# Two layers of row scatters that skip nodes which are no edge's source, with the tables zeroed during the sorts

## The reference, cut to what matters

```python
loops = jnp.arange(N); src = concat([edge_index[0], loops]); dst = concat([edge_index[1], loops])
deg = segment_sum(ones, dst, N); dinv = rsqrt(deg); norm = dinv[src] * dinv[dst]
for l in range(3):
    h = x @ W[l].T
    agg = segment_sum(h[src] * norm[:, None], dst, N) + b[l]
    xn = (agg - mean(agg, 0)) * rsqrt(var(agg, 0) + 1e-5)
    x = relu(gamma[l] * xn + beta[l])
x = layernorm(x0 + x)
x = layernorm(x + messages(x, src, dst, edge attributes))
```

## Time and profile before

| | us |
|---|---|
| device time, median of 3 runs | 1859.32 |
| the three runs | 1864.98, 1859.32, 1850.93 |
| the profiled execution: span | 1724.5 |
| the profiled execution: device time of its own | not listed |
| the sorts, from the span's start to the last issue on SyncE's queue | 0 to 178.5 |
| the page's slices | 43.1 each |

### The profile page before, as it was taken

How to read it: one execution, slowest core, us unless ns; L and a number is a source line. 1 busy time by engine, 2 the same in 40 slices (tenths; PEclk the granted TensorE clock), 3 DMA queues, 4 the chain that set the end, 5 groups by cost and what they waited for, 6 DMA issues and landing times. The chain is left out here.

```text
span 1724.5 us, 26873 instructions
## 1 busy us (share of the span) xinstructions
PE 1368.7 (79%) x8020; PEld 1171.3 (68%) x8020; DVE 1213.7 (70%) x3500; ACT 905.4 (53%) x1796; POOL 889.3 (52%) x865
## 2 busy tenths in 40 slices
PE   4566599999988799999979999964444459999941
PEld 3455488788877688888868888853333358888831
DVE  7257566655656577777758777857877669999873
ACT  3462234433434577777566666635665644444374
POOL 5770567777774678777552343302333533433226
PEclk8799699999999899999989999975666679999955
DMA  2000697777867676777664566448998733333113
GB/s 62 2 2 2 220 315 253 256 257 253 271 226 261 209 246 246 249 258 258 222 202 158 202 206 207 151 186 290 337 343 326 302 85 91 85 93 90 55 45 142
DMA packets 129803, 330.41 MB, mean 192 GB/s; under 512 B 33772, under 2 KB 66020, under 8 KB 126870
## 3 DMA queue, kind: packets, MB, share of 16 engines
q1 hardware_dynamic: 79766, 185.96, 30.7%
q0 software_dynamic: 49920, 143.05, 25.7%
HBM read 166.44 MB, written 166.95 MB: 193 GB/s over the span
## 5 line engine op out<-in xcount | busy, mean ns | idle before, releaser
L1048 PE MATMUL ps_b<-yhi,whi 128*128 128x492 f32 (+1 forms) x960 | 398.5, 415 | 19.7 <-ACT aggT L940 15.1
L1048 PE MATMUL ps_b<-ylo,whi 128*128 128x492 f32 (+1 forms) x960 | 379.6, 395 | 0.0
L1048 PE MATMUL ps_b<-yhi,wlo 128*128 128x492 f32 (+1 forms) x960 | 379.3, 395 | 0.0
L940 ACT COPY aggT<-ps_b 128x492 f32<-128x492 f32 (+1 forms) x240 | 137.9, 575 | 313.6 <-PE ps_b L1048 313.3
L858 DVE BATCH_NORM_STATS2 stat<-aggT 128x6 f32<-128x492 f32 (+1 forms) x240 | 162.1, 678 | 147.0 <-ACT aggT L940 146.9
L700 POOL DMA_INDIRECT rows<-rows_out,node_at x160 | 187.3, 1170 | 108.9 <-ACT rows_out L946 60.9
L1048 PEld LDWEIGHTS ps_b<-yhi,whi 128*128 128x128 f32 x960 | 186.0, 194 | 51.1 <-ACT aggT L940 15.5
L1048 PEld LDWEIGHTS ps_b<-yhi,wlo 128*128 128x128 f32 x960 | 184.9, 193 | 38.6
L1048 PEld LDWEIGHTS ps_b<-ylo,whi 128*128 128x128 f32 x960 | 186.1, 194 | 30.5 <-issue 0.5
L1176 POOL DMA_INDIRECT out<-fin_out,node_at x80 | 79.2, 991 | 185.1 <-DVE fin_out L1245 94.9
L707 POOL TENSOR_TENSOR X<-X,own_row 128x1016 f32<-128x1016 f32 x40 | 96.4, 2411 | 131.6 <-ACT X L924 131.3
(11 more groups left out here) (366 smaller groups left out, 3069.7 us busy)
## 6 DMA issues: line engine op xcount, KB each, us to landing
z<-aggT SPq DMA_DIRECT2D x30, 1016.0 KB, 5.5
z<-aggT SPq DMA_DIRECT2D x30, 984.0 KB, 8.4
x_rows<-R SPq DMA_DIRECT2D x80, 256.0 KB, 4.3
fin_xr<-x_rows SPq DMA_DIRECT2D x20, 1024.0 KB, 9.0
X<-z SPq DMA_DIRECT2D x20, 1016.0 KB, 8.2
X<-z SPq DMA_DIRECT2D x20, 984.0 KB, 7.7
x<-fin_x SPq DMA_DIRECT2D x10, 1024.0 KB, 10.7
fin_X<-z SPq DMA_DIRECT2D x10, 1016.0 KB, 14.1
```

The source lines that it names most:

```text
L940: nc.scalar.copy(f.aggT[t % 2][:, j, 0:cols(t)], f.ps_b[j % 2][:, 0:cols(t)]).then_inc(x["copied"], 1)
L1048: o = nc.tensor.matmul(f.ps_b[j % 2][:, 0:n], w[:, c, j * P:(j + 1) * P], y[g % 2][:, c, 0:n], start=(c == 0 and i == 0), stop=(c == C - 1 ...
```

## The change

The scatter of layers 0 and 1 takes its rows' indices from a new table, `table_at`: the node, plus `SKIP` if the node is no edge's source. VectorE fills it block by block in layer 0 with two operations on 128 x 4 (`aim`). The rows that are not written any more keep zeros: both tables are filled during the sorts by two DMAs on SyncE's queue, from a tile `blank` of 125 partitions and 512 zeros, read 80 times by each; SyncE waits for them at the end of the sorts.

```diff
-def order_edges(m, k, s, a):
+def order_edges(m, k, s, a, table):
...
+    zeroed, blank_in = m.sem("ord_zeroed"), m.sem("ord_blank_in")
...
                 sp.dma_start(s.rawW[i][:], a.W[i].rearrange("(c p) f -> p c f", p=P)).then_inc(w_in[i], 16)
+            sp.wait_ge(zeroed, 1)
+            for rows in table:
+                rows = rows.rearrange("(p t) f -> p t f", p=k.blank.shape[0])
+                sp.dma_start(rows, k.blank[:].unsqueeze(1).to_broadcast(list(rows.shape))).then_inc(blank_in, 16)
             sp.wait_ge(made, 5)
...
             sp.wait_ge(end_in, 16)
+            sp.wait_ge(blank_in, 32)
...
             nc.vector.memset(k.eps[:], LN_EPS)
+            nc.vector.memset(k.blank[:], 0.0).then_inc(zeroed, 1)
...
                 pool.wait_ge(x["rows"], 4 * (layer * NB + b) + j + 1)
-                pool.indirect_dma_start(table[layer], bass.IndirectOffsetOnAxis(ap=k.node_at[:, i, 0:1], axis=0), f.rows[j][:], None,
+                pool.wait_ge(x["aimed"], min(layer * NB + b, NB - 1) + 1)
+                pool.indirect_dma_start(table[layer], bass.IndirectOffsetOnAxis(ap=k.table_at[:, i:i + 1], axis=0), f.rows[j][:], None,
                                         bounds_check=m.N - 1, oob_is_err=False).then_inc(put[j], 16)
...
+            def aim(b):
+                if m.edges(b):
+                    dve.wait_ge(id_in[m.nth(b) % 2], 64 * (m.nth(b) // 2 + 1))
+                at = slice(m.tile(b, 0)[0], m.tile(b, 0)[0] + 4)
+                nc.vector.tensor_scalar(k.unread[:, at], k.node_at[:, at, 1], 0.5, float(SKIP), ALU.is_lt, ALU.mult).then_inc(x["unread"], 1)
+                dve.wait_ge(x["unread"], b + 1)
+                nc.vector.tensor_tensor(k.table_at[:, at], k.node_at[:, at, 0], k.unread[:, at], ALU.add).then_inc(x["aimed"], 1)
...
                     build(m.nth(t + 3))
+                if layer == 0 and runs(t):
+                    aim(t)
...
+            k.table_at, k.unread, k.blank = m.sb("table_at", [P, 2 * ET], I32), m.sb("unread", [P, 2 * ET]), m.sb("blank", [125, d])
...
-                order_edges(m, k, s, a)
+                order_edges(m, k, s, a, table)
```

More of the change, by code:

```diff
@@ L592, in graph_layers @@
              "turned", "edge_x", "plain_x", "act_x", "shifted", "relued", "weighted", "merged", "carried", "joined",
-             "hi", "lo", "product", "copied", "counted", "back", "rows", "zero", "tabled", "cont")
+             "hi", "lo", "unread", "aimed", "product", "copied", "counted", "back", "rows", "zero", "tabled", "cont")
     x = {n: m.sem(f"gcn_{n}") for n in names}
```

## The result

The changed kernel takes **1936.8 us** (median of 4 runs, 1935.3 to 1942.0) where the kernel before, with the run measured beside it, takes 1861.7 (4 runs, 1850.9 to 1865.0): 1.0439 of its time, with a 95% interval of 1.039 to 1.0487. Slower was predicted, and it is slower; but 2021 us were predicted and at least 1978, and the loss is 75 us instead of 162.

A forecast was written before the change was run, and what follows sets the result against it. Sorts were bounded by a chain of small VectorE and TensorE steps ending on SyncE, layers by TensorE (with gaps in the first). Span 1724.5 + 176.5 - 15 = 1886.0, plus 134.8, gave 2021 us; 8 in 10: 1978 to 2090 us.

The forecast's parts named there:

- The fill: In the sorts, two DMAs on SyncE's queue write 40.96 MB on five engines at 122.7 GB/s: 334 us, ending at 352 us.
- the tail of 3 us: On SyncE's queue after the fill: column stores and read-back, 2.5 us, plus two issues of 0.3 us.
- The rivals of sixteen, ten, one or slower engines: Fill in the sorts: sixteen engines 1844 us (0.07), ten 1854 (0.02), one 3357 (0.02), five slower ones 2102 (0.11).
- The sorts end at 355 us in place of 178.5 us: +176.5 us.: End of the sorts: the fill and the steps queued behind it delay the barrier by 176.5 us.
- what lies around its span ... 134.8 us: Outside the profiled span: the listed runs' median, 1859.3 us, less the span of 1724.5 us, added to the forecast unchanged.
- the +200 in the stated range: Upper fill term in the forecast's own range, 1978 to 2065 us (+153 - 34 to +200 + 5), given 0.78.
- the bound worked out for five slow engines: Fill in the sorts at a busy engine's 20.5 GB/s: 400 us, +243 us; as a rival 2102 us, chance 0.11.
- The scatters, "-15 us": First layer: unsent rows, 12.46 MB fewer per layer, shrink the DMA backlog and give back 15 us, 34 at most.
- ScalarE's 48.0 us of waiting for scatters: First layer: ScalarE's waits for a previous scatter, taken to lie mostly beside TensorE's products and not added.
- TensorE's 19.0 us for gathered rows: First layer: weight loads' waits for gathered source rows, counted in the 34 us at most that the skip could return.
- The new operations, "I take 0": First layer: two VectorE operations a block and GpSimd's wait for them stay hidden; 8 us if cover is gone.
- The second layer, "0": Second layer: TensorE is busy 203.00 of 203 us, with no gap to close, so the skip gains 0.

The follow-up runs named there:

- first profile: Kernel before, unchanged, as profiled ahead of the prediction: span 1724.5 us, sorts end at 178.5 us; its own device time is not on record.
- second profile: Kernel before, unchanged, profiled again with the experiments: span 1866.2 us, sorts end at 277.5 us, median time 1868.0 us.
- the two kernels with the faster fill: Changed kernel with the blank tile on 80 partitions, not 125: 1819.8 us with skipped rows, 1819.0 us with scatters of all rows.
- third profile of before: Kernel before, unchanged, profiled once more: span 1854.9 us, sorts end at 278.3 us, median time 1856.7 us.

## Why the prediction was right, and where it was wrong

**The fill: right, within 8 us.** Five engines were read from the load of the attributes, 122.7 GB/s were taken and 127 are there; 352 us were given for its end and it ends between 340 and 346 us; the tail of 3 us is about 6, and in it the read-backs wait for the column stores to land. By the Trainium skill (DMA: Bandwidth & Descriptors, section "Why a DMA increments its semaphore by 16 and not by 1") a tile of 125 partitions against 10000 rows runs on 5 engines, and one of 80 on 16. The 0.33 of the engines busy on 125, and 0.88 in the kernel with 80 (below), agree with it. The rivals of sixteen, ten, one or slower engines are out.

**The step that failed: "The sorts end at 355 us in place of 178.5 us: +176.5 us."** The first number stands (346.9), the second does not. In the executions that were timed the sorts before end at 277.5 us, so the same fill adds 69 us. The 99 us between are waits that the first profile doesn't have: beside GpSimd's scatters at 1.28 us for one, VectorE and ScalarE lose up to 17 us at a time, ScalarE once 30 and TensorE once 55. That the scatters cause them is shown by the kernels that move or thin them: the positions then end at 149 to 193 us instead of 248. In the changed kernel what is left of these waits lies under the fill and costs nothing. So the step took the baseline of the sorts, and with it the overlap, from an execution that was not the timed one, and counted as loss 99 us that the timed kernel spends waiting anyway.

**The warning that was passed over: "what lies around its span ... 134.8 us".** That a kernel spends 135 us outside its first and last instruction was an assumption by which a shorter execution was made to fit the timed ones. In the runs where both are known the distance is 1.7 us (1941.95 us with a span of 1940.2 for the changed kernel, 1867.95 with 1866.2 for before). Of the 141.7 us between the two spans of before, 98.9 are in the sorts, 34.1 in the layers and 8.7 behind them. The prediction added its 176.5 us to all of them as if the change could not touch them; 99 of them are waits of the sorts that the fill now covers. What the 34 us in the layers are was not tried: the second profile has waits on "remote" there too (ScalarE 58.7 us and VectorE 52.0 in the window from 325 to 665 us), and the first has none. A slip beside it changes little: the +200 in the stated range comes from no sum, where the bound worked out for five slow engines is +243.

**The scatters, "-15 us": nothing that the times show.** The bytes are saved as predicted. GpSimd's queue in the first layer's 340 us, in the second profile of before and after:

```profile
q0 software_dynamic: 14470, 43.17, 39.7%
```

```profile
q0 software_dynamic: 14495, 32.89, 32.4%
```

A quarter of the queue's bytes goes. A scatter takes 1092 ns instead of 1192 in that window, but that is not the skip: with the same fill and all rows it takes 1089. The first layer is as long, 392.3 us after 392.7 (from ScalarE's first copy to `aggT` in it to the first in the next layer). Among the kernels with the new operations it takes 392.3, 397.0 and 397.8 us with the skip and 400.0 and 401.6 with all rows, so a few us may be there that the new operations take back. ScalarE's 48.0 us of waiting for scatters do not appear in the second profile of before, nor TensorE's 19.0 us for gathered rows as a wait for a DMA (the same line has 12.3 us there without a named cause). They belonged to the first profile. Leaving out all rows gave some 9 us between the medians, less than the 15 that were given to leaving out 61% of them.

**The new operations, "I take 0": likely about +10 us.** They were said to cost 8 us if their cover were gone, and the first layer of the kernel without them is 9.7 us shorter. GpSimd itself waited for them 2.2 to 5.0 us in the first layer of the two kernels with the faster fill, so most of it would be what stands behind them on VectorE.

**The second layer, "0":** 203.00 of 203 us of TensorE became 196.43 after, and 198.66 in the same window of the second profile of before; nothing was won there.

## What to carry to other kernels

Hold the span of a profile against the timed runs before building on its stages: here they differ by 1.7 us where both are known, and by some 135 where the stages that were read were not those that are timed; a sum made on them was off by what the missing time hid. Look at the number of partitions of a fill's tile: 125 left it a third of the DMA engines here, and with 80 the kernel with the fill was faster than the kernel without it. Do not take back-to-back indirect DMAs on GpSimd to be free for the other engines where GpSimd is off the path: allow fewer in flight and measure. With two instead of four this kernel is 3.6% faster than before, with neither the skip nor the fill.

## What the runs showed of the hardware that was not expected

- Beside scatters of 128 x 8 B every 1.28 us, VectorE stood for up to 16 us and ScalarE for up to 30 with their inputs ready; at 1.52 us the positions lost 37 us in all, at 2.95 us 2 us. The scatters' transfers themselves did not suffer: the load that waits for them is issued at 133.5 and 133.4 us in the first two profiles of before. By what path GpSimd's DMAs delay the other engines, why ScalarE stands some 10 us behind the last of them, and why the execution of the first profile was spared at the same rate, stays open. Code loading is one path that was not tried: from 47 to 128 us the queues that load instructions moved nothing in the second and third profile of before, and nine packets in the first, and whether that is a cause or a consequence of the engines' standing was not tested.
- A fill from 80 partitions keeps the engines busy but is slower than the 391 GB/s of the earlier trace rows: 295 GB/s at first, then 234, in the windows of that kernel:

```profile
20.00:40.00 20.00, 12.93 (x115) 11.25 (x116) 13.89 (x71) 10.66 (x28) 4.06 (x4) 0.83 1.02 295
40.00:120.00 80.00, 50.34 (x338) 40.82 (x335) 27.05 (x228) 38.24 (x118) 26.16 (x27) 0.66 0.88 234
```

That is 16.6 GB/s for a busy engine (234 / 0.88 / 16), where the fill on five has 24.1 (127 / 0.33 / 16). Why was not tried.
